# Perceiver layer, sixteen tiles on one core: x also comes transposed, its mean is taken out of q's weights, its deviation goes into q's masks, and self attention scores are made in two halves

## The reference

```python
x = x + _L0_xattn_ref(_layernorm(x), ctx_2048, mask, norm_w, wq, wk, wv, wo, wg)
x = x + _L0_attn_ref(_layernorm(x), w_qkv, w_proj, q_gain)
x = x + _L0_ffn_ref(_layernorm(x), w1, w2, w3)
# in _L0_xattn_ref: 16 heads of 16, softmax over 257 rows
x = rmsnorm(hidden_states, norm_w)
q = (x @ wq.T).reshape(B, L, NH, HD)
attn = jnp.einsum('blhd,bmhd->bhlm', q, k) * scale
gate = jax.nn.sigmoid(x @ wg.T)
return gate * (out @ wo.T)
```

## Time and profile before

| what | value |
|---|---|
| median of the runs | 559.83 us (559.17 to 559.93, 3 runs) |
| the profiled execution | 561.7 us, span 559.9 us |
| PE, DVE, ACT, POOL busy | 95%, 79%, 74%, 54% of the span |
| granted TensorE clock | 0.999 |

### The profile page before, as it was taken

The page is one execution under the profiler, slowest core; times in us unless marked ns, Lnnn a source line. Parts: engine busy times, 40 slices in busy tenths (PEclk is TensorE's granted clock), DMA queues, the critical chain, the costliest instruction groups (busy, mean ns, idle before and its releaser), DMA issues. The chain is left out here.

```text
span 559.9 us, 19727 instructions
## 1 busy us (share of the span) xinstructions
...
## 2 busy tenths in 40 slices
...
GB/s 247 187 97 184 77 71 48 109 47 91 43 72 86 76 86 71 87 33 100 53 73 87 80 87 62 92 44 83 59 74 87 107 67 4 59 21 8 31 12 9
DMA packets 42801, 42.16 MB, mean 75 GB/s; under 512 B 16080, under 2 KB 33488, under 8 KB 42704
## 3 DMA queue, kind: packets, MB, share of 16 engines
...
## 5 line engine op out<-in xcount | busy, mean ns | idle before, releaser
L894 ACT ACTIVATE pr<-sm,nb 128x257 f32<-128x257 f32 x256 | 129.6, 509 | 24.7 <-DVE nb L1130 24.6
L1130 DVE CUSTOM_DVE_ANT_0 sm<-x_ps,mbias 128x257 f32<-128x257 f32 x256 | 99.5, 417 | 16.8 <-PE x_ps L1448 10.8
L671 POOL TENSOR_TENSOR cTl<-cx,cTh 128x512 fp32r<-128x512 f32 x64 | 84.3, 1325 | 35.8 <-ACT cTh L783 35.6
L783 ACT ACTIVATE pt<-x_ps 128x512 f32<-128x512 f32 x112 | 66.3, 595 | 12.7 <-PE x_ps L1458 12.4
L1458 PE MATMUL x_ps<-tab,pr 128*128 128x128 f32 x512 | 73.2, 275 | 0.4 <-DVE nb L1130 0.4
L1458 PEld LDWEIGHTS x_ps<-tab,pr 128*128 128x128 f32 x512 | 59.6, 141 | 9.3 <-issue 1.0
L677 POOL TENSOR_SCALAR rv<-mv 128x1 f32<-128x1 f32 x32 | 6.4, 200 | 100.5 <-DVE mv L994 91.8
L679 POOL TENSOR_TENSOR sr<-sv,halfneg 128x20 f32<-128x20 f32 x16 | 56.7, 3543 | 1.3
L1328 PE MATMUL x_ps<-wvTh,cTh 128*128 128x256 f32 x256 | 56.8, 303 | 0.0
L783 ACT ACTIVATE vv<-x_ps 128x512 f32<-128x512 f32 x64 | 38.0, 593 | 19.7 <-PE o_ps L1473 13.2
L1328 PE MATMUL x_ps<-wvTh,cTl 128*128 128x256 f32 x256 | 51.3, 282 | 0.0
...
## 6 DMA issues: line engine op xcount, KB each, us to landing
...
```

What stands on the lines that cost most here:

```text
L671: g.tensor_tensor(cT[1][:, :, b % BT, :], cx[:, b % BT, :, :], cT[0][:, :, b % BT, :].bitcast(F32), ALU.subtract).then_inc(A_ctl, 1)
L783: return sc.activation(dst, src, ACT.Copy)
L894: sc.activation(pr[:, b % 2, gr, :], sm[:, b % 2, gr, :], ACT.Exp, bias=nb[:, n:n + 1], scale=-1.0, accum_out=st[:, 0, b, gr:gr + 1]).then ...
L1130: v.tensor_tensor_reduce(out=sm[:, b % 2, gr, :], in0=xb(f"S{b}", gr)[:, 0:LK], in1=mbias[:, b, :], scale=1.0, scalar=0.1 * NEG, op0=ALU.a ...
```

## The change

The host also passes x transposed (`x_t`). Since the mean over features can be taken out of the weights, each column of `wqT` and `wgT` loses its mean once (`column_sums` on TensorE, `centre` on DVE), and q and the gate are products with x itself. The deviation comes in later: as the scale of the gate's tanh per row, and for q, whose rows lie along the free axis, as the mask `rsm`. POOL's root `rsq` is stored to memory (`RS`) and read back to all partitions by eight DMAs (`RB`); `q_blocks` waits for all of them. `Q_norm` and `Q_h` go, with the copy to `hT`. In self attention q and k of sequences 0 and 1 lie on partitions 0 to 63 and of 2 and 3 on 64 to 127; `D_QT` and `D_kT` are products with half of the identity, `D_S` alternates the two halves of the rows and fills two banks, and DVE adds the causal mask in two instructions. All banks and lists are new; the "each" lists of PE, DVE, POOL and SP are shown, those of ACT and the "first" and "last" parts are left out. There, SP's list has `RB` ahead of `B_shuffle` (periods 0 to 2, and 14).

```diff
-    "B_qkv": (5,), "D_QT": (1,), "D_kT": (3,), "D_S": (1,), "D_PV": (4,), "D_yT": (3,), "D_pj": (1,), "C_xT":
...
+    "B_qkv": (5,), "D_QT": (3,), "D_kT": (1,), "D_S": (0, 1,), "D_PV": (5,), "D_yT": (6,), "D_pj": (5,), "C_xT":
...
         "each": [
-            ("S", 0), ("B_st",), ("C_xT",), ("D_QT",), ("D_kT",), ("V", 1), ("D_S",), ("S", 1), ("B_O",),
-            ("C_z", 0), ("K", 1, 0), ("B_oT",), ("K", 1, 1), ("PT", 0, 0), ("B_wo",), ("PT", 0, 1), ("V", 2),
-            ("S", 2), ("PV", 0), ("PT", 1, 0), ("PT", 1, 1), ("GATE",), ("B_xT",), ("C_z", 1), ("S", 3), ("B_qkv",),
-            ("C_z", 2), ("PV", 1), ("D_PV",), ("Q_h",), ("V", 3), ("PT", 2, 0), ("D_yT",), ("K", 2, 0),
-            ("PT", 2, 1), ("Q_q",), ("C_hT",), ("D_pj",), ("PV", 2), ("C_y",), ("K", 2, 1), ("PT", 3, 0),
-            ("PT", 3, 1), ("V", 4), ("PV", 3),
+            ("S", 0), ("B_st",), ("C_xT",), ("D_QT",), ("D_kT",), ("V", 1), ("D_S",), ("S", 1), ("C_z", 0),
+            ("B_O",), ("K", 1, 0), ("B_oT",), ("K", 1, 1), ("B_wo",), ("PT", 0, 0), ("S", 2), ("PT", 0, 1),
+            ("V", 2), ("PV", 0), ("B_xT",), ("PT", 1, 0), ("PT", 1, 1), ("C_z", 1), ("B_qkv",), ("C_z", 2),
+            ("S", 3), ("PV", 1), ("D_PV",), ("V", 3), ("D_yT",), ("Q_q",), ("K", 2, 0), ("K", 2, 1), ("C_hT",),
+            ("PT", 2, 0), ("PT", 2, 1), ("D_pj",), ("C_y",), ("GATE",), ("PT", 3, 0), ("PV", 2), ("PT", 3, 1),
+            ("V", 4), ("PV", 3),
         ],
...
         "each": [
-            ("D_scale",), ("S", 0, 0), ("S", 0, 1), ("B_den",), ("D_kT",), ("B_o1",), ("S", 0, 2), ("S", 0, 3),
-            ("B_comb",), ("B_comb2",), ("D_S",), ("B_O",), ("S", 1, 0), ("B_fin",), ("D_mx",), ("S", 1, 1),
-            ("S", 1, 2), ("S", 1, 3), ("C_z", 0), ("D_s3",), ("Q_stats",), ("B_wo",), ("B_x1",), ("D_dn",),
-            ("C_h", 0), ("S", 2, 0), ("S", 2, 1), ("S", 2, 2), ("B_norm",), ("D_p3",), ("S", 2, 3), ("Q_norm",),
-            ("B_xT",), ("D_p4",), ("S", 3, 0), ("C_z", 1), ("S", 3, 1), ("C_h", 1), ("S", 3, 2), ("C_z", 2),
-            ("B_qkv",), ("C_h", 2), ("C_q", 0), ("C_q", 1), ("S", 3, 3), ("D_yT",), ("C_q", 2), ("PT", 2, 1),
-            ("C_y",), ("D_pj",), ("D_xstats",), ("D_xq", 0), ("D_xq", 1), ("D_xq", 2),
+            ("D_scale",), ("S", 0, 0), ("B_den",), ("S", 0, 1), ("S", 0, 2), ("D_kT",), ("B_o1",), ("S", 0, 3),
+            ("B_comb",), ("B_comb2",), ("D_S",), ("S", 1, 0), ("B_O",), ("S", 1, 1), ("B_fin",), ("D_mx",),
+            ("Q_stats",), ("S", 1, 2), ("S", 1, 3), ("C_z", 0), ("D_s3",), ("B_wo",), ("B_x1",), ("S", 2, 0),
+            ("C_h", 0), ("B_norm",), ("S", 2, 1), ("D_dn",), ("S", 2, 2), ("B_xT",), ("S", 2, 3), ("D_p3",),
+            ("D_p4",), ("C_z", 1), ("C_h", 1), ("C_z", 2), ("B_qkv",), ("C_h", 2), ("S", 3, 0), ("S", 3, 1),
+            ("S", 3, 2), ("C_q", 0), ("S", 3, 3), ("C_q", 1), ("C_q", 2), ("D_yT",), ("PT", 2, 1), ("C_y",),
+            ("D_pj",), ("D_xstats",), ("D_xq", 0), ("D_xq", 1), ("D_xq", 2),
         ],
...
         "each": [
-            ("CL", 2), ("CL", 3), ("CL", 4), ("PX", 0), ("B_root",), ("PX", 1), ("CL", 5), ("Q_root",), ("B_rope",),
-            ("D_yroot",), ("B_qkroot",), ("QBD", 0), ("PX", 2), ("QBD", 1), ("QBD", 2), ("D_xroot",), ("PX", 3),
-            ("QBD", 3), ("EX",),
+            ("CL", 2), ("CL", 3), ("CL", 4), ("B_root",), ("PX", 0), ("PX", 1), ("CL", 5), ("Q_root",), ("B_rope",),
+            ("B_qkroot",), ("PX", 2), ("QBD", 0), ("QBD", 1), ("D_yroot",), ("QBD", 2), ("PX", 3), ("QBD", 3),
+            ("EX",), ("D_xroot",),
         ],
...
         "each": [
-            ("LCTX", 0), ("LMB", 0), ("LCTX", 1), ("LX",), ("LCTX", 2), ("LMB", 1), ("LCTX", 3), ("B_shuffle",),
-            ("LMB", 2), ("LVX",), ("LMB", 3), ("LXR",), ("C_store",),
+            ("LCTX", 0), ("LX",), ("LCTX", 1), ("LCTX", 2), ("LMB", 0), ("LMB", 1), ("LXT",), ("RS",),
+            ("B_shuffle",), ("LCTX", 3), ("RB",), ("LMB", 2), ("C_store",), ("LMB", 3), ("LXR",), ("LVX",),
         ],
...
+            def load_xt(i):
+                sp.dma_start(xT[:, i % 2, :, :].rearrange("p k c -> p (k c)"), x_t[i]).then_inc(L_xt, 16)
...
+            def keep_rs(i):
+                sp.wait_ge(Q_r, i + 1)
+                if due(8 * i):
+                    sp.wait_ge(L_rs, 128 * i)
+                sp.dma_start(rs_dram, rsq[:, i % 2]).then_inc(L_rsw, 16)
+
+            def spread_rs(i):
+
+                sp.wait_ge(L_rsw, 16 * i + 16)
+                if due(i - 1):
+                    sp.wait_ge(Q_bd, 4 * i - 4)
+                else:
+                    sp.wait_ge(W_rz, 1)
+                for n in range(P // HD):
+                    sp.dma_start(rsm[n * HD:(n + 1) * HD, i % 2, n % HP, :], rs_dram.partition_broadcast(HD)).then_inc(L_rs, 16)
+
             load_x(0, xq, L_xq)
...
+            load_xt(0)
...
+            keep_rs(0)
             load_ctx(0, 1)
+            spread_rs(0)
             load_w(3, wg, L_w)
             sp.dma_start(woT[:, :, :], wo).then_inc(L_w, 16)
             for b in range(2, BT):
...
                     elif k == "LX":
-                        sp.wait_ge(Q_hn, i + 1)
+                        sp.wait_ge(Q_mv, i + 1)
                         load_x(i + 1, xq, L_xq)
+                    elif k == "LXT":
+                        if due(i):
+                            sp.wait_ge(A_gp, i)
+                        if due(i):
+                            sp.wait_ge(Q_qp, i)
+                        load_xt(i + 1)
+                    elif k == "RS":
+                        keep_rs(i + 1)
+                    elif k == "RB":
+                        spread_rs(i + 1)
...
             def q_root(i):
 
-                root(i, Q_mv, i + 1, mvq[:, 1:2], rvq[:, :], rsq[:, :], 1.0 + RMS_EPS, LN_EPS * RMS_EPS, Q_v, Q_r)
+                if due(i - 1):
+                    pool.wait_ge(A_g, i - 1)
+                    pool.wait_ge(L_rsw, 16 * i - 16)
+                root(i, Q_mv, i + 1, mvq[:, 1:2], rvq[:, :], rsq[:, i % 2:i % 2 + 1], 1.0 + RMS_EPS, LN_EPS * RMS_EPS, Q_v, Q_r)
 
             def q_blocks(i, b):
 
                 pool.wait_ge(Q_qh, i + 1)
+                pool.wait_ge(L_rs, 128 * i + 128)
                 if due(16 * i + 4 * b - 12):
                     pool.wait_ge(A_ttr, 16 * i + 4 * b - 12)
                 if b % 2 == 0:
...
                     pool.wait_ge(A_ke, 2 * i + b // 2 + 1)
                 g.tensor_tensor(qbd[:, :, b, :, :],
                                 qT[:, :, b * S:(b + 1) * S].unsqueeze(2).to_broadcast([P, 2, HP, S]),
-                                qm.unsqueeze(1).unsqueeze(3).to_broadcast([P, 2, HP, S]), ALU.mult).then_inc(Q_bd, 1)
+                                rsm[:, i % 2, :, b * S:(b + 1) * S].unsqueeze(1).to_broadcast([P, 2, HP, S]), ALU.mult).then_inc(Q_bd, 1)
...
             def q_hi(i, ps):
                 act.wait_ge(Q_qp, i + 1)
                 if due(4 * i):
                     act.wait_ge(Q_bd, 4 * i)
-                copy(qT[:, :, :], ps[:, 0:D].rearrange("p (k c) -> p k c", k=2)).then_inc(Q_qh, 1)
+                sc.activation(qT[:, :, :], ps[:, 0:D].rearrange("p (k c) -> p k c", k=2), ACT.Copy, scale=-float(HD) ** -0.5).then_inc(Q_qh, 1)
...
                         for k2 in range(2):
-                            last = sc.activation(wgT[:, k2, :], wraw[:, 3, k2, :], ACT.Copy, scale=nwc[:, k2:k2 + 1])
+                            last = sc.activation(wgT[:, k2, :], wraw[:, 3, k2, :], ACT.Copy, scale=nwh[:, k2:k2 + 1])
                         last.then_inc(W_ev, 1)
...
-                        sc.activation(gt[:, :], xb("GATE")[:, 0:D], ACT.Tanh, scale=0.5).then_inc(A_g, 1)
-                    elif k == "Q_h":
-                        q_hT(i + 1, xb("Q_h"))
+                        act.wait_ge(Q_r, i + 1)
+                        sc.activation(gt[:, :], xb("GATE")[:, 0:D], ACT.Tanh, scale=rsq[:, i % 2:i % 2 + 1]).then_inc(A_g, 1)
...
-            def q_norm(i):
-                dve.wait_ge(Q_r, i + 1)
-                if due(i):
-                    dve.wait_ge(Q_hTp, i)
-                v.tensor_scalar(hn[:, :], xq[:, :], mvq[:, 0:1], rsq[:, :], ALU.subtract, ALU.mult).then_inc(Q_hn, 1)
+            def centre(w, ps, done):
+
+                v.scalar_tensor_tensor(out=w[:, :, :], in0=ps[:, 0:D].unsqueeze(1).to_broadcast([P, 2, D]), scalar=-1.0 / D,
+                                       in1=w[:, :, :], op0=ALU.mult, op1=ALU.add).then_inc(done, 1)
 
...
                         copy(qTs[:, :, :, :].rearrange("p b h q -> p h b q"),
-                             xb("D_QT")[0:64, :].rearrange("p (h b q) -> p h b q", h=4, b=BT)).then_inc(B_qTs, 1)
+                             xb("D_QT")[:, 0:D].rearrange("p (h b q) -> p h b q", h=4, b=2)).then_inc(B_qTs, 1)
...
                     elif k == "D_S":
                         dve.wait_ge(B_sp, i1)
-                        v.tensor_tensor(s2[:, :, :], xb("D_S")[:, :].rearrange("p (j k) -> p j k", k=S),
```

(41 more changed lines are left out.)

308 lines of the change are left out of this document (149 added, 159 removed), and 107 rows, old and new, of tables (BANK, SCHEDULE).

## The result

The changed kernel takes 698.13 us, the median of four executions from 687.75 to 703.66, against 559.88 us before. Two of these four, the profiled one among them, are slow executions, over 1.5% above the fastest, so the ratio of 1.2349 (95% interval 1.2185 to 1.2514) is that of the other two, whose mean is 692.3 us. The forecast was 579.5 us in a range of 554 to 588. The direction was right, and the size was off by a factor of seven: +138 us instead of +20. The profile is of the 703.66 us execution, span 701.9 us. From the first `D_QT` to the fourteenth it took 408.98 us before and takes 525.12 us now (+116.1, thirteen distances). The head before the first is 26.0 us longer (96.77 against 70.76), what follows the fourteenth 0.2 us shorter. That adds up to 142.0, the difference of the spans.

What follows compares the result with a forecast made beforehand. A steady tile was taken as bound by TensorE's work plus a VectorE/GpSimd chain, with GpSimd held by the broadcasts. From 561.7: +17.5 loop, +4 head, −2 tail gives 581.2; less 1.9, 579.5 us, range 554 to 588.

Steps and rivals of the forecast that it cites:

- its landing is waited for until 278.04: 1.88: SP's queue, each steady tile: the wait for v's store to land before the four scatters, 1.88 us.
- `D_QT` to `B_qkv`: TensorE's stretch with GATE and S3 moved out, `D_S` shorter and `D_QT` longer: from 15.29 to 13.42 us.
- L: Time from `B_qkv` until all eight broadcasts have landed for `q_blocks`: 11.1 us, between 10.5 and 11.5.
- to `D_xroot`: GpSimd's work from the broadcasts' landing to the root of x: four blocks, y root, `PX` and `EX`, 4.0 us.
- to `D_QT`: From the root of x on GpSimd to the next `D_QT` on TensorE: 4.65 us.
- The head, +4: First tiles: the deviations' trip delays SP's later loads and the mask's store; +4 us, bounds −1 and +7.
- The clock stays at 1.00, so no price here depends on it.: TensorE's granted clock, read from the profile before: taken as 1.00, with no term for a lower clock.
- TensorE's work, −0.59: Per steady tile: `Q_h` gone −0.20, `D_S` in halves −0.54, `D_QT` as matmuls +0.15; 30.37 to 29.8 us.
- `D_kT`, four passes, comes out even: TensorE, each tile: dividing `D_kT` into halves was priced at no change.
- The tail, −2: Tiles 14 and 15 gain some 0.5 us each, two draining tiles 0.54 in `D_S`: −2 us, bounds −4 and +2.
- Not held (555.5): Rival, chance 0.22: broadcasts land before GpSimd is free; period 31.0 us with the 7.40 us chain, −0.6 a tile.
- The two conditions that I named for being wrong: Prediction wrong if the steady period is below 31.6 us (L about 9 or less) or idle time stands at another wait.

Runs made afterwards that it cites:

- e2_wide_store: The changed kernel with the deviations' store writing 128 pieces of 256 bytes from a constant tile instead of 4 bytes; every wait kept: 593.93 us.
- e1_no_trip: The changed kernel without the deviations' store, its waits and the eight broadcasts; a constant mask instead, deviation left out of q: 545.03 us, ratio 0.9697.
- e10_store_alone_spaced: The kernel before plus an unread store of the deviations ahead of v's store in tiles 1 to 14, 4-byte pieces 256 bytes apart: 561.0 us, ratio 1.0015.
- e7_fillers: The changed kernel with unread matmuls in TensorE's two long waits in tiles 3 to 13 (12 before `B_st`, 30 before `C_xT`): 692.03 us.
- e12_one_rsm: The changed kernel with deviations spread on chip by a matmul and two activations instead of through memory, `rsm` in one buffer: 548.78 us, ratio 0.9783.
- e11_no_halves: The changed kernel with deviations spread on chip, `D_QT`, `D_kT` and `D_S` in their old undivided form, `rsm` in one buffer: 552.69 us, ratio 0.9867.
- e4_rb_first: The changed kernel with the eight broadcasts moved ahead of `B_shuffle` in SP's "each" order: 658.76 us, ratio 1.1748.
- e5_on_chip: The changed kernel with the deviations spread on chip by one matmul and two activations instead of through memory, output complete: 548.83 us, ratio 0.9781.

## Why the prediction was wrong, step by step

**The step that failed: v's landing, "its landing is waited for until 278.04: 1.88".** I took the duration of v's landing for a queue that now has another store ahead of it. It is 7.19 us. The loop as forecast and as measured, in the changed kernel from `D_QT` 337.69 through `B_qkv` 353.23, kk 370.43 and the root 374.15 to the next `D_QT` 378.66:

| part of the loop | forecast | changed kernel | e2_wide_store |
|---|---|---|---|
| `D_QT` to `B_qkv` | 13.42 | 15.54 | 15.21 |
| `B_qkv` to first kk (L) | 11.1 | 17.20 | 11.31 |
| to `D_xroot` | 4.0 | 3.72 | 3.74 |
| to `D_QT` | 4.65 | 4.51 | 3.72 |
| period | 33.17 | 40.97 | 33.98 |

Where the store lands in 2 us, L comes out at 11.31 and the period within 0.81 us of the forecast; the whole kernel takes 593.9 us instead of 579.5. So the mechanism was right, the trip behind `B_shuffle` holding GpSimd and through it the root, and one term of it was mis-sized by 5.3 us. That is most of the 7.8 us by which the period is too long; 2.1 are the way from `D_QT` to `B_qkv`, now at the low clock, and 0.7 the issue and landing of the broadcasts. The bounds of L, 10.5 to 11.5, were the worse fault: I had no row of a store of 4 bytes for each partition, and took both bounds from rows with long pieces. An honest upper bound wasn't to be had from that trace, and the range should have said so. Nor did the text price the landing of `RS` itself in the steady tile at all; it entered the head alone, as "a wait of 2 to 4 us".

**The head, +4.** It is +26.0 in the changed kernel and 75.40 − 70.76 = +4.6 with the wide store. But e1_no_trip, without any trip, has 73.80, +3.0: only 1.6 of the 4.6 are the trip's, little more than the 1.3 between two kernels that do the same up to there (70.76 before, 69.44 in e10_store_alone_spaced). The +4 was met by luck. The trip does shift the mask's first read by 5.6 us with the wide store (18.63 against 13.00), as forecast; TensorE's first `D_QT` hardly feels it. With the packed store the read comes 10.7 us later and the first `D_QT` 26.0; how the one becomes the other I did not follow.

**"The clock stays at 1.00, so no price here depends on it."** That was read from the kernel before, whose stalls are 1.2 us. With stalls of 1.55 and 3.87 us it falls to 0.50 for 4.7 us. `D_QT` to `B_qkv` takes 13.67 us at full clock (e1_no_trip, 253.99 to 267.66), near my 13.42, and 15.1 to 16.3 in most tiles with the stalls. Even the forecast's own stall costs 1.5 us a tile there: in e2_wide_store TensorE waits 2.23 us at one place, and nine tiles take 15.1 to 15.2 us. The way from the root to `D_QT`, 0.93 us shorter than I had it, gives part of it back. In all its profiled execution, 589.11 us, misses the 581.2 of the sum by 7.9: the loop has +23.0 instead of +17.5, the head +4.6 instead of +4, the tail −0.2 instead of −2. e7_fillers warns that taking the low clock away need not give the time back.

**TensorE's work, −0.59.** `D_S` fell by 0.45 instead of 0.54; `D_QT` rose by 0.05 instead of 0.15 (0.51 us in e12_one_rsm, 283.40 to 283.91). The term that I had at nothing without a reason, "`D_kT`, four passes, comes out even", is what was missing:

```profile
283.91 0.29 PE L1591 MATMUL x_ps<-tab,rqk 128*64 128x64 f32 x4
284.13 0.51 PE L1364 MATMUL x_ps<-wvTh,cTh 128*128 128x256 f32 x2
```

It takes 0.22 us to the next start, and undivided in e11_no_halves 0.03 (286.67 to 286.70). So the halves save about 0.2 us of TensorE's work, as e11_no_halves against e12_one_rsm says too (30.46 − 30.24), not 0.39. Fully busy, the tile of e1_no_trip has 30.01 us against 30.36 before, −0.35 in all. The direction held, and the size was 0.24 too hopeful.

**The tail, −2.** It is −0.2.

**"Not held (555.5)".** e1_no_trip is this rival, and it takes 545. My 31.0 a tile kept the chain of 7.40 us from `C_y` to `D_QT`. It is 284.00 − 277.67 = 6.33 us there: VectorE's rqk takes 482 ns instead of 1344, and its xf 0.41 us instead of 0.61. Before:

```profile
L1216 DVE TENSOR_TENSOR rqk<-rc,srg x16: 491/1344/1356, 67.9 to 526.2; 128x320 f32<-128x320 f32 x16
```

In e1_no_trip:

```profile
L1248 DVE TENSOR_TENSOR rqk<-rc,srg x16: 480/482/491, 72.1 to 511.4; 128x320 f32<-128x320 f32 x16
```

The traces show what decides. In the kernel before GpSimd starts cTl at 289.27, and rqk starts at 289.54, while cTl runs: 1.34 us. Where no cTl runs beside it (476.28) rqk takes 0.49 in the same kernel. In the new order it takes 0.48 as a rule, but one tile of e4_rb_first has cTl ahead again:

```profile
161.90 1.26 POOL L709 TENSOR_TENSOR cTl<-cx,cTh 128x512 fp32r<-128x512 f32 x1 [1.98 <-ACT cTh L825]
162.15 1.36 DVE L1251 TENSOR_TENSOR rqk<-rc,srg 128x320 f32<-128x320 f32 x1
```

And where rqk starts first, an overlap costs it nothing (changed kernel):

```profile
620.77 0.48 DVE L1251 TENSOR_TENSOR rqk<-rc,srg 128x320 f32<-128x320 f32 x1
620.84 1.55 POOL L709 TENSOR_TENSOR cTl<-cx,cTh 128x512 fp32r<-128x512 f32 x1
```

So it is a cTl already under way that makes rqk slow, in either order. The Trainium skill, VectorE: DVE Perf Modes, Two Vector instructions with no wait between them, says that what such an instruction reads as its second input comes over an interface that VectorE shares with GpSimd; these rows agree, and the page gives no price for it.

This also says where the gain of 12 us in e5_on_chip (560.79 to 548.83) comes from: 3.9 us from the halves, and the other 8 from what else changed. The stall of 1.2 us a tile is gone, which I put down to the new order and the shorter chain; no run has the new order alone. The dropped `Q_h` (0.20 us) about pays for the new matmul.

**What bounds it, and the signs to look for.** GpSimd's idle time stood where I had put it, before the first kk copy, and TensorE's before `C_xT` and `B_st`, behind the root; they were 8.58 us instead of 2 to 3, and 3.87 and 1.55 instead of 3.4 in all. The two conditions that I named for being wrong (a period below 31.6, another wait) did not come for the loop that sets the period; the error was one that I had not listed, the same wait three times as long.
